# Cross-attention scores of a row tile: four chunks of 362 keys in two halves, or three chunks of 484 with a maximum each

## The chip, the cores and the metric

The kernel runs on one core of a Trainium2 chip. Its metric is the device time of one execution in microseconds; the median of three executions is compared. TensorE (PE) does the matrix products and transposes, VectorE (DVE) and ScalarE (ACT) work on what it leaves in PSUM, GpSimd (POOL) works in SBUF only, and SyncE (SP) starts the transfers. The engines run their own instruction streams and meet at semaphores.

## What is computed

A pre-norm decoder block over 16 samples of 100 tokens, width 128: banded self-attention, cross-attention over 1444 context keys with 16 heads, and a mixture of 16 experts with top 2 and a shared expert. The change lies in the cross-attention:

```
Q = (x @ W_Q.T + b_Q) per head;  K, V = (ctx @ W_K.T + b_K), (ctx @ W_V.T + b_V)
scores = where(mask, -10000, Q K^T / 8)         # 16 x 16 heads x 100 queries x 1444 keys
x = x + softmax(scores) V @ W_out.T + b_out
```

## The kernel before

The key projection is folded into the queries, so that all heads share the 128-wide context as keys and as values. A sample's 1600 rows (100 queries by 16 heads) make 13 row tiles: `FT` = 12 of 128 rows and one of 64 (`probs_half`). The keys are padded to `SKP` = 1448 columns. Each number is split in a high and a low part (`_hi`, `_lo`, type fp32r), and three products stand for one.

For a row tile t:

- **score** (PE, `score`, L1019): scores go to four PSUM banks, 362 keys in each, in two halves of two banks. A half is six matmuls: hi by hi, hi by lo, lo by hi, for two banks each. 26 halves for a sample.
- **take** (DVE, L943): one instruction for a half adds the bias row (mask and a constant), negates into `probs`, and carries the minimum so far (`nmax`), 724 elements in a row. The second half starts from the first one's minimum. A small read of the accumulator follows each.
- **bias** (POOL, L824): made for tile t + 1 while tile t is scored; two buffers.
- **exp** (ACT, L880) over the 1448 elements, with their sum; **recip** (DVE, L950) of the sum; **norm** (POOL, L836) multiplies the row by it.
- **step** (PE): two tiles form a group (the last group has three), which is taken in steps: transposes of two key blocks (`turn`, L1036) to one of two banks, ACT copies them as the high part `pT_hi` (L889), DVE makes the low part `pT_lo` (L955), and three steps later PE multiplies them with the context (`values`, L1061). 42 steps for a sample. At a group's end ACT and DVE take its result (`oT_hi`, L895, and `oT_lo`, L961). The first `turn` of group g waits until all its tiles are normalized.
- **prep** and **project**: queries and keys of the next sample, and the output projection of the one before.

All of it is one software pipeline over samples. `period()` writes out the order of one period by hand: steps 27 to 41 of the sample before, then steps 0 to 26 of this one, spread by their costs over the range 0 to 1; scores spread evenly in it (half n at (n + 0.5)/26); then preps at given places. PE follows that list. The lists of the other engines are the same with offsets in entries of it: exp at 1.5 entries after the last score entry of its tile, recip at 3.6, norm at 4.6, a take at 0.2 after its score, `pT_lo` at 0.5 after its step. Every engine works its list strictly in order. The hardware loop holds two periods (`odd` 1 and 0); its loads and register waits are repeated for each.

The end and the beginning of a period read, on PE, before: ... step 25, score 12.1, step 26 | step 27, score 0.0, step 28, score 0.1, step 29, step 30, score 1.0 ... (score t.h is half h of tile t). Step 30 is the first of the group with tiles 10, 11 and 12 of the sample just scored. Within a step PE first multiplies (values of three steps before), then transposes.

After the cross-attention come the experts (L1536 to L1552 are their matmuls, 400 columns each).

## Time and profile before

| | |
|---|---|
| median of 3 executions | 1850.08 us (1842.12 to 1850.58) |
| profiled execution, span from first to last instruction | 1843.5 us |
| around the span | no time of the profiled execution by itself is shown; the median of the runs is 6.6 us above its span |
| cross-attention, first to last score | 134.8 to 1485 us |
| PE busy, and DVE, ACT, POOL | 93%, 68%, 53%, 53% of the span |

Matmul records have an estimated end, so what a matmul costs is read from one start to the next. "xN" in a timeline row are N instructions in a row, with the start of the first. In brackets stands how long the engine was idle before, and what ended that.

### The profile page before, as it was taken

The numbers are of one execution on the slowest core, as the hardware profiler recorded it, in microseconds if no ns is written. First come the engines' busy times: TensorE is split into PE (matmuls) and PEld (weight loads), VectorE is DVE, ScalarE is ACT, GpSimd is POOL, SyncE is SP. The second block draws the span as 40 slices with busy tenths as digits, with TensorE's granted clock in tenths as the row PEclk, the third lists the DMA queues.
The fourth block names the chain that finished last, engine by engine and source line by source line (L and its number), as shares of the span: only waits on it lengthen the run. The fifth ranks groups of instructions, "written<-read, shape, count | busy, mean of one in ns | idle before, by whom it ended". The sixth has DMA issues, their size and how long they took to land. (4 is left out here: it accounts for less than half of the span.)

```text
span 1843.5 us, 37864 instructions
## 1 busy us (share of the span) xinstructions
PE 1708.8 (93%) x11436; PEld 1611.8 (87%) x11436; DVE 1262.3 (68%) x2678; ACT 978.6 (53%) x1763; POOL 975.0 (53%) x838
## 2 busy tenths in 40 slices
PE   5569999999999999999999999999999985899998
PEld 5448999989999998999899989999999974888887
DVE  5727776757676766677676757675767645788887
ACT  1216555646555655555555646464655532566665
POOL 0037565646465655556465646464656410666665
PEclk9769999999999999999999999999999996999999
DMA  5032010101010111101010101010100001222221
GB/s 84 1 92 62 25 52 29 45 30 48 31 48 27 51 36 41 49 29 48 27 52 29 47 27 48 31 48 27 51 29 29 24 22 55 79 79 79 79 79 44
DMA packets 89712, 83.69 MB, mean 45 GB/s; under 512 B 16003, under 2 KB 87069, under 8 KB 89519
## 3 DMA queue, kind: packets, MB, share of 16 engines
q1 hardware_dynamic: 82816, 79.03, 13.7%
q10 hardware_dynamic: 6703, 2.28, 0.9%
q8 instruction: 98, 1.61, 0.3%
q14 instruction: 95, 0.78, 0.1%
HBM read 77.08 MB, written 4.21 MB: 44 GB/s over the span
## 5 line engine op out<-in xcount | busy, mean ns | idle before, releaser
L955 DVE TENSOR_TENSOR pT_lo<-banks,pT_hi 128x512 fp32r<-128x512 f32 (+1 forms) x672 | 420.2, 631 | 307.1 <-ACT pT_hi L889 304.0
L889 ACT CAST pT_hi<-banks 128x512 fp32r<-128x512 f32 (+1 forms) x672 | 361.1, 543 | 429.2 <-PE banks L1036 422.2
L836 POOL TENSOR_SCALAR probs<-probs,row_inv 128x1448 f32<-128x1448 f32 x192 | 283.8, 1478 | 245.6 <-DVE row_inv L950 245.4
L824 POOL TENSOR_SCALAR bias<-mask,c_cur 128x1444 f32<-128x1444 uint8 x192 | 283.0, 1474 | 201.7 <-DVE nmax L943 189.0
L1036 PE MATMUL banks<-ident,probs 128*128 128x128 f32 x2304 | 363.3, 273 | 10.2 <-POOL probs_half L836 8.2
L1061 PE MATMUL banks<-pT_hi,ctx_hi 128*128 128x256 f32 (+1 forms) x1152 | 358.2, 311 | 12.8 <-DVE pT_lo L955 12.3
L1061 PE MATMUL banks<-pT_hi,ctx_lo 128*128 128x256 f32 (+1 forms) x1152 | 331.5, 288 | 0.0
L1061 PE MATMUL banks<-pT_lo,ctx_hi 128*128 128x256 f32 (+1 forms) x1152 | 330.1, 287 | 0.0
L880 ACT ACTIVATE probs<-probs,nmax 128x1448 f32<-128x1448 f32 x192 | 289.8, 1509 | 36.7 <-DVE nmax L943 36.7
L1036 PEld LDWEIGHTS banks<-ident,probs 128*128 128x128 f32 x2304 | 275.2, 141 | 15.9 <-issue 11.4
L1291 POOL TENSOR_TENSOR gated<-hid,gate_rows 128x400 f32<-128x400 f32 x144 | 172.1, 1202 | 145.7 <-DVE hid L1470 144.7
L1019 PE MATMUL banks<-ctxT_hi,qh 128*128 128x362 f32 x832 | 242.8, 373 | 4.4 <-POOL ql L858 2.8
L1061 PEld LDWEIGHTS banks<-pT_hi,ctx_hi 128*128 128x128 f32 x1152 | 219.8, 191 | 24.2 <-issue 14.5
L1061 PEld LDWEIGHTS banks<-pT_lo,ctx_hi 128*128 128x128 f32 x1152 | 219.3, 190 | 0.0
L1061 PEld LDWEIGHTS banks<-pT_hi,ctx_lo 128*128 128x128 f32 x1152 | 218.5, 190 | 0.0
L1019 PE MATMUL banks<-ctxT_hi,ql 128*128 128x362 f32 x832 | 207.7, 331 | 0.0
L1019 PE MATMUL banks<-ctxT_lo,qh 128*128 128x362 f32 x832 | 207.5, 331 | 0.0
L943 DVE CUSTOM_DVE_ANT_0 probs<-banks,bias,nmax 128x724 f32<-128x724 f32 x192 | 185.1, 964 | 14.2 <-PE banks L1019 12.8
L943 DVE CUSTOM_DVE_ANT_0 probs<-banks,bias 128x724 f32<-128x724 f32 x192 | 174.1, 907 | 27.4 <-PE banks L1019 16.5
L1461 DVE TENSOR_TENSOR h_lo<-gated,h_hi 128x400 fp32r<-128x400 f32 x144 | 133.1, 925 | 38.1 <-ACT h_hi L1350 38.0
L1019 PEld LDWEIGHTS banks<-ctxT_lo,qh 128*128 128x128 f32 x832 | 149.6, 191 | 0.0
L1019 PEld LDWEIGHTS banks<-ctxT_hi,ql 128*128 128x128 f32 x832 | 149.3, 191 | 0.0
(207 smaller groups left out, 2802.2 us busy)
## 6 DMA issues: line engine op xcount, KB each, us to landing
mask<-in_mask_BxSxS_bk SPq DMA_DIRECT2D x192, 180.5 KB
gate_rows<-gates_dram SPq DMA_DIRECT2D x18, 800.0 KB, 4.1
nat<-in_ctx SPq DMA_DIRECT2D x16, 704.0 KB
w_raw<-in_L_ffn_W SPq DMA_DIRECT2D x48, 128.0 KB, 2.1
mask_half<-in_mask_BxSxS_bk SPq DMA_DIRECT2D x16, 90.2 KB
xt<-in_x SPq DMA_DIRECT2D x4, 200.0 KB
x_dram<-xt SPq DMA_DIRECT2D x4, 200.0 KB
n2hi_dram<-n2hi SPq DMA_DIRECT2D x4, 200.0 KB
```

What stands on the lines that cost most here:

```text
L824: pool.tensor_scalar(bias[(t + i) % 2][0:n, 0:SK], src[:, :], MASKED, c_cur[i][0:n, t:t + 1], ALU.mult, ALU.add).then_inc(bias_ready, 1)
L836: pool.tensor_scalar(prob(j)[0:n, :], prob(j)[0:n, :], rinv[0:n, s:s + 1], 1.0, ALU.mult, ALU.mult).then_inc(probs_ready, 1)
L880: act.activation(prob(j)[0:n, :], prob(j)[0:n, :], ACT.Exp, bias=nmax[0:n, 1, s:s + 1], scale=-1.0, accum_out=rsum[0:n, s:s + 1]).then_inc ...
L889: act.copy(pT_hi[tslot(i, j)][:, 0:w], banks[:, T_BANK + j % 2, 0:w]).then_inc(turned_hi, 1)
L943: dve.tensor_tensor_reduce(prob(t)[0:n, cs].rearrange("p (a k) -> p a k", a=2), src, bias[(t + i) % 2][0:n, cs].rearrange("p (a k) -> p a ...
L955: dve.tensor_tensor(pT_lo[tslot(i, j)][:, 0:w], banks[:, T_BANK + j % 2, 0:w], pT_hi[tslot(i, j)][:, 0:w].bitcast(F32), ALU.subtract)\
L1019: last = pe.matmul(banks[:, S_BANK + c, 0:CW], qpart[:, rows], kpart[:, c * CW:(c + 1) * CW], start=first, stop=qpart is ql[i])
L1036: last = pe.transpose(banks[:, T_BANK + j % 2, at_col:at_col + r], prob(t)[0:r, c0:c0 + 128], ident[0:r, 0:r])
L1061: last = pe.matmul(banks[:, out_bank(g), 0:w], stationary[:, k, :], moving[tslot(i, j)][:, cs], start=(k == 0 and stationary is ctx_hi[i] ...
L1291: pool.tensor_tensor(gated[:, n % 4, :], hid[n % 2][:, :], gate_rows[odd][:, c * CT:(c + 1) * CT], ALU.mult).then_inc(gated_done, 1)
L1461: dve.tensor_tensor(h_lo[bodd][:, m, cs], gated[:, bn % 4, :], h_hi[bodd][:, m, cs].bitcast(F32), ALU.subtract).then_inc(hlo_done, 1)
```

## The change

A row tile's scores are taken in three parts of 484, 482 and 482 keys instead of two halves of 724. Each part lies in one bank, and the parts go round four banks. PE issues three matmuls for a part (nine for a tile, twelve before), and each part has a take of its own with its own `nmax` column. PE may start part n when part n - 4 is taken (before: half n when half n - 2 is taken); at the first two parts of every second sample, where the bank numbering starts anew, it waits for more. Scores are now 39 entries of the period instead of 26, which has 93 entries instead of 80; the offsets of exp, recip and norm stay 1.5, 3.6 and 4.6 entries after the tile's last score entry.

```diff
-CW = 362
-SKP = 4 * CW
+PARTS = [slice(0, 484), slice(484, 966), slice(966, 1448)]
+NP = len(PARTS)
+SKP = 1448
...
-    for n in range(2 * NT):
-        out.append(((n + 0.5) / (2 * NT), "score", 0, n))
+    for n in range(NP * NT):
+        out.append(((n + 0.5) / (NP * NT), "score", 0, n))
...
-        if kind == "score" and j % 2:
-            out.append((n + 1.5, "exp", db, j // 2))
+        if kind == "score" and j % NP == NP - 1:
+            out.append((n + 1.5, "exp", db, j // NP))
...
-            if j % 2:
-                out.append((n + 3.6, "recip", db, j // 2))
+            if j % NP == NP - 1:
+                out.append((n + 3.6, "recip", db, j // NP))
...
-        if kind == "score" and j % 2:
-            out.append((n + 4.6, "norm", db, j // 2))
+        if kind == "score" and j % NP == NP - 1:
+            out.append((n + 4.6, "norm", db, j // NP))
...
-        nmax = sb("nmax", [128, 2, PSLOTS + 1])
+        nmax = sb("nmax", [128, NP, PSLOTS + 1])
...
+        S_BANKS = 4
+
+        def score_bank(b_odd, n):
+            return S_BANK + (NP * NT * b_odd + n) % S_BANKS
...
-                            cs = slice(half * 2 * CW, (half + 1) * 2 * CW)
-                            src = banks[0:n, S_BANK + 2 * half:S_BANK + 2 * half + 2, 0:CW]
-                            first = -PAD if half == 0 else nmax[0:n, 0, s:s + 1]
+                            cs = PARTS[part]
+                            src = banks[0:n, score_bank(i, j), 0:cs.stop - cs.start]
+                            first = -PAD if part == 0 else nmax[0:n, part - 1, s:s + 1]
...
-                    wait(pe, scores_taken, b, 2 * NT, n - 1)
+                    wait(pe, scores_taken, b, NP * NT, n - 1 if i == 0 and n < 2 else n - S_BANKS + 1)
+                    cs = PARTS[part]
                     for qpart, kparts in ((qh[i], (ctxT_hi[i], ctxT_lo[i])), (ql[i], (ctxT_hi[i],))):
                         for kpart in kparts:
                             first = qpart is qh[i] and kpart is ctxT_hi[i]
-                            for c in (2 * half, 2 * half + 1):
-                                last = pe.matmul(banks[:, S_BANK + c, 0:CW], qpart[:, rows],
-                                                 kpart[:, c * CW:(c + 1) * CW], start=first, stop=qpart is ql[i])
+                            last = pe.matmul(banks[:, score_bank(i, n), 0:cs.stop - cs.start], qpart[:, rows],
+                                             kpart[:, cs], start=first, stop=qpart is ql[i])
                     last.then_inc(scores_ready, 1)
```

The waits on `scores_taken` and `scores_ready` of the other engines count 39 for a sample instead of 26, in the same sense.

## Rows read from the trace of the kernel before

**Rows 1.** The page: busy us, share of the span and instructions of each engine.

```profile
PE 1708.8 (93%) x11436; PEld 1611.8 (87%) x11436; DVE 1262.3 (68%) x2678; ACT 978.6 (53%) x1763; POOL 975.0 (53%) x838
```

**Rows 2.** Busy time by engine in two consecutive periods; clock, DMA share, GB/s last.

```profile
398.00:482.00 84.00, 83.91 (x605) 80.57 (x605) 59.22 (x136) 48.56 (x86) 49.85 (x41) 1.00 0.13 40
482.00:570.00 88.00, 85.44 (x604) 81.89 (x603) 59.30 (x135) 48.48 (x86) 49.87 (x41) 0.98 0.13 39
```

**Rows 3.** Waits over the whole span: us in total, times, longest us.

```profile
PE banks L1061 <- DVE pT_lo L955: 12.3, 6, 2.2
PE banks L1036 <- POOL probs_half L836: 8.2, 7, 2.2
```

**Rows 4.** Timeline at a period's change inside the loop: PE alone.

```profile
805.29 0.58 PE L1019 MATMUL banks<-ctxT_hi,qh 128*128 128x362 f32 x2
...
806.37 0.28 PE L1061 MATMUL banks<-pT_hi,ctx_hi 128*128 128x256 f32 x1
...
807.08 0.60 PE L1036 MATMUL banks<-ident,probs 128*128 128x128 f32 x4
807.43 0.57 PE L1019 MATMUL banks<-ctxT_hi,qh 128*128 128x362 f32 x2
807.84 0.49 PE L1019 MATMUL banks<-ctxT_lo,qh 128*128 128x362 f32 x2
...
808.51 0.28 PE L1061 MATMUL banks<-pT_hi,ctx_hi 128*128 128x256 f32 x1
```

**Rows 5.** Timeline of PE among the experts: seven matmuls of 400 columns.

```profile
1701.17 0.34 PE L1536 MATMUL banks<-t_hi,w_hi 128*128 128x400 f32 x1
...
1702.44 0.34 PE L1551 MATMUL banks<-h_lo,w_hi 128*128 128x400 f32 x1
```

**Rows 6.** Groups by line and shape: count, busy us, mean ns of one.

```profile
L955 DVE TENSOR_TENSOR pT_lo<-banks,pT_hi 128x512 fp32r<-128x512 f32 x480 | 327.4, 687 | 194.3 <-ACT pT_hi L889 191.2
L943 DVE CUSTOM_DVE_ANT_0 probs<-banks,bias,nmax 128x724 f32<-128x724 f32 x192 | 185.1, 964 | 14.2 <-PE banks L1019 12.8
L943 DVE CUSTOM_DVE_ANT_0 probs<-banks,bias 128x724 f32<-128x724 f32 x192 | 174.1, 907 | 27.4 <-PE banks L1019 16.5
L955 DVE TENSOR_TENSOR pT_lo<-banks,pT_hi 128x320 fp32r<-128x320 f32 x192 | 92.8, 490 | 112.8 <-ACT pT_hi L889 112.8
...
L943 DVE DVE_READ_ACCUMULATOR2_ANT nmax<- 128x1 f32 x384 | 31.8, 83 | 0.0
```

**Rows 7.** Timeline of the same change of period: the last score and what follows it.

```profile
801.98 0.58 PE L1019 MATMUL banks<-ctxT_hi,qh 128*128 128x362 f32 x2
...
803.77 0.60 PE L1036 MATMUL banks<-ident,probs 128*128 128x128 f32 x4
...
804.13 0.95 DVE L943 CUSTOM_DVE_ANT_0 probs_half<-banks,bias,nmax 64x724 f32<-64x724 f32 x1
...
805.13 1.51 ACT L880 ACTIVATE probs_half<-probs_half,nmax 64x1448 f32<-64x1448 f32 x1
...
805.64 0.41 DVE L961 TENSOR_TENSOR oT_lo<-banks,oT_hi 128x256 fp32r<-128x256 f32 x1
...
807.84 0.90 DVE L943 CUSTOM_DVE_ANT_0 probs<-banks,bias 128x724 f32<-128x724 f32 x1
...
808.66 0.15 DVE L950 RECIPROCAL row_inv<-row_sum 64x1 f32<-64x1 f32 x1
...
810.26 0.28 PE L1061 MATMUL banks<-pT_hi,ctx_lo 128*128 128x256 f32 x1
...
810.62 0.43 PE L1036 MATMUL banks<-ident,probs 128*128 128x128 f32 x2
```

**Rows 8.** Timeline where the loop starts anew (the period before that one).

```profile
718.43 0.38 PE L1061 MATMUL banks<-pT_hi,ctx_hi 128*128 128x256 f32 x1 [2.20 <-DVE pT_lo L955]
...
719.93 0.42 DVE L961 TENSOR_TENSOR oT_lo<-banks,oT_hi 128x256 fp32r<-128x256 f32 x1 [2.35 <-issue]
...
726.49 0.43 PE L1036 MATMUL banks<-ident,probs 128*128 128x128 f32 x2 [1.64 <-POOL probs_half L836]
```

More of the change, by code:

```diff
@@ L173, in pool_order @@
     for n, kind, db, j in ORDER:
-        if kind == "score" and j % 2 == 0:
-            t = j // 2 + 1
+        if kind == "score" and j % NP == 0:
+            t = j // NP + 1
             out.append((n + 0.5, "bias", db if t < NT else db + 1, t % NT))
-        if kind == "score" and j % 2:
-            out.append((n + 4.6, "norm", db, j // 2))
+        if kind == "score" and j % NP == NP - 1:
+            out.append((n + 4.6, "norm", db, j // NP))
         elif kind == "prep" and j >= 3:
@@ L820, in make_bias @@
                             wait(pool, mask_half_in, b + db, 16, 16)
-                        wait_apart(pool, scores_taken, b + db, 2 * NT, 2 * (t - 1), passed_pool)
+                        wait_apart(pool, scores_taken, b + db, NP * NT, NP * (t - 1), passed_pool)
                         src = masks[t % MSLOTS] if t < FT else mask_half
@@ L877, in emit @@
                             n, s = rows_of(j), slot(j)
-                            wait(act, scores_taken, b + db, 2 * NT, 2 * j + 2)
+                            wait(act, scores_taken, b + db, NP * NT, NP * j + NP)
                             act.activation(prob(j)[0:n, :], prob(j)[0:n, :], ACT.Exp,
-                                           bias=nmax[0:n, 1, s:s + 1], scale=-1.0,
+                                           bias=nmax[0:n, NP - 1, s:s + 1], scale=-1.0,
                                            accum_out=rsum[0:n, s:s + 1]).then_inc(exp_done, 1)
@@ L923, in emit @@
                         if kind == "score":
-                            t, half = j // 2, j % 2
+                            t, part = j // NP, j % NP
                             n, s = rows_of(t), slot(t)
-                            if half == 0:
+                            if part == 0:
                                 wait(dve, bias_ready, b + db, NT, t + 1)
@@ L935, in emit @@
                             else:
-                                wait(dve, scores_taken, b + db, 2 * NT, j)
-                            wait_apart(dve, scores_ready, b + db, 2 * NT, j + 1, passed_dve)
-                            cs = slice(half * 2 * CW, (half + 1) * 2 * CW)
-                            src = banks[0:n, S_BANK + 2 * half:S_BANK + 2 * half + 2, 0:CW]
-                            first = -PAD if half == 0 else nmax[0:n, 0, s:s + 1]
+                                wait(dve, scores_taken, b + db, NP * NT, j)
+                            wait_apart(dve, scores_ready, b + db, NP * NT, j + 1, passed_dve)
+                            cs = PARTS[part]
+                            src = banks[0:n, score_bank(i, j), 0:cs.stop - cs.start]
+                            first = -PAD if part == 0 else nmax[0:n, part - 1, s:s + 1]
                             dve.tensor_tensor_reduce(
-                                prob(t)[0:n, cs].rearrange("p (a k) -> p a k", a=2), src,
-                                bias[(t + i) % 2][0:n, cs].rearrange("p (a k) -> p a k", a=2), -1.0, first,
-                                ALU.add, ALU.min, nmax[0:n, half, s:s + 1]).then_inc(scores_taken, 1)
+                                prob(t)[0:n, cs], src, bias[(t + i) % 2][0:n, cs], -1.0, first,
+                                ALU.add, ALU.min, nmax[0:n, part, s:s + 1]).then_inc(scores_taken, 1)
                         elif kind == "recip":
@@ L1006, in score @@
                 def score(b, i, n):
-                    t, half = n // 2, n % 2
+                    t, part = n // NP, n % NP
                     rows = slice(t * 128, (t + 1) * 128)
```

## The prediction

> **What bounds the kernel now.** I read the page first: PE is busy 93% of the span, the next engine, DVE, 68% [rows 1]. A busy PE need not be a full PE, so I cut the span into periods of one sample. One takes 84 us, with PE busy 83.9 of them; the next takes 88 with PE busy 85.4, and TensorE's clock is 1.00 and 0.98 of full [rows 2]. So the even kind is work of PE from end to end, and the odd kind has some 4 us more. The list of waits says what they are: PE waited for DVE's `pT_lo` six times in the whole run, 12.3 us, and for the norm of `probs_half` seven times, 8.2 us [rows 3]. Those are the turns of the loop, where engines have nothing to run for a while (DVE's 2.35 us end with "issue" [rows 8]). Elsewhere the low parts are always made in time. A change of this kernel is therefore worth what it does to PE's own stream, and to the few places where PE stands; all else is hidden until it makes PE stand.
>
> **PE's stream.** A score matmul of 362 columns starts 0.1675 us after the one before: (808.51 - 807.84)/4 [rows 4]. With 256 columns it is (807.08 - 806.37)/6 = 0.118 [rows 4], with 400 columns, three after one another into the same bank, (1702.44 - 1701.17)/7 = 0.181 [rows 5]. Going from 256 to 400 adds 0.44 ns a column, so nearly all of the price is columns, and the change leaves those alone: 12 x 362 and 484 + 482 + 482 three times are both 4344. What is saved is the fixed part of three matmuls. A matmul of 484 columns is not in the trace. Bounds: in proportion to 362 columns 0.224; with the slope from 362 to 400, 0.36 ns a column, 0.212. I take 0.220, a little above the 0.219 that is in proportion to 400 columns, its nearest row. For a tile: 12 x 0.1675 = 2.010 before, 9 x 0.220 = 1.98 after, 0.03 less; for 208 tiles 6 us less (bounds: nothing, and 21 us less). Every matmul has a weight load of the same size, and at 256 columns these still fit into 0.118 [rows 4]; fewer of them save nothing by themselves.
>
> The Trainium skill ("TensorE: Matmul & The Clock Gate", Back-to-back issue gap) gives N/2.4 + 2.5 ns for an isolated gap; an estimate by it is 153 and 204 ns, some 8 ns less for a tile, 2 us in all. The same section states about 81 ns at 128 columns and 131 at 512 in a real stream; the rows of 362 and 400 columns disagree with that, and by it the change would be worth tens of microseconds, which is the second rival.
>
> The switch between transposes and split products costs 1.08 - 6 x 0.1675 = 0.08 us after each `turn`, whoever comes next [rows 4]; there are 42 turns in a period before and after, so 13 more score entries add no switch. Four banks give PE three parts ahead, so its own wait on `scores_taken` is not tighter, save for the first parts of every second sample. There part 0.0 needs part 12.1 taken, which by the chain below may be some 0.3 us late; it precedes the stall told next and is mostly taken back out of that.
>
> **DVE.** A take of 724 costs 907, or 964 ns if it starts from a maximum, and each is followed by a read of the accumulator (83 ns). `pT_lo` shows the price per element, (687 - 490)/192 = 1.03 ns [rows 6]. So 484 cost 907 - 240 x 1.03 = 0.66 us, and 482 with a maximum 964 - 242 x 1.03 = 0.715. For a tile: 0.66 + 2 x 0.715 + 3 x 0.083 = 2.34 after, 0.907 + 0.964 + 0.166 = 2.04 before. That is 0.3 us more for each of 208 tiles, 63 us of DVE in all; in a period DVE goes from 59 to 63 of 84 us [rows 2]. The cover is its idle time, 25 us a period, and parts come more evenly than halves did, about one between two steps. Behind a take on DVE stands the next `pT_lo`, and PE waits for that at the second step after. I price it at nothing; if the cover is gone at one step of every period it costs what is missing there, some 0.5 us, 8 us in all.
>
> **The one chain without slack.** Step 30 transposes the group of tiles 10 to 12, and tile 12 was scored last. In the undisturbed change of period PE's last value product starts at 810.26, the transposes would follow 0.12 later, and they start at 810.62: 0.24 late, for the norm [rows 7]. The links are: the take of 12.1 starts 804.13, exp 1.00 later, at 805.13; the take of 0.0 at exp + 2.71 (it stands on DVE behind `pT_lo` of step 27, which stands behind exp on ACT), recip at exp + 3.53, the transposes, with the norm on POOL between, at recip + 1.96 [rows 7].
>
> Now the new order, worked out from the fractions: ... step 25, score 12.1, step 26, score 12.2 | 0.0, step 27, 0.1, step 28, 0.2, step 29, step 30. The last score has moved behind step 26, and 0.0 ahead of step 27. Count PE from the start of 12.2. A part is 0.66, after a turn 0.74; a step after a score 1.06 (807.43 - 806.37), its values alone 0.71 [rows 4]. The transposes of step 30 come due at 0.74 + 0.66 + 1.06 + 0.74 + 1.06 + 0.74 + 1.06 + 0.08 + 0.71 = 6.85. Before, they came due 8.64 - 0.24 = 8.40 after the start of 12.1 at 801.98 [rows 7]. The deadline is 1.55 us nearer.
>
> The chain shortens less. The take of 12.2 stands on DVE behind `pT_lo` of step 26 and the `oT_lo` that ends group 3 there. `oT_lo` ends 806.05 - 803.77 = 2.28 after the start of step 26's transposes [rows 7], and those start 0.35 before part 12.2, so the take starts at 1.9, exp 0.75 later (a shorter take) at 2.65. Recip's offset, 3.6 entries, now puts it behind the take of 0.1, not of 0.0; that take is 0.2 shorter, so recip is at exp + 3.35 and the transposes at exp + 5.3 = 7.95. They are 1.1 late instead of 0.24. Bounds: if the take of 12.2 goes ahead 0.4 us sooner, 0.7; if 0.1 waits once more behind something, 1.8. I take 0.85 more in each undisturbed period, eight with the last sample: 7 us.
>
> At the loop's turn the same chain carries DVE's stop as well: 2.35 us before `oT_lo`, another before the take of 0.0, and PE then waits 1.64 us for the norm [rows 8]. By the sum of waits that is 8.2/7 = 1.2 us each [rows 3]. Of the nearer deadline 0.85 stays here too unless the stop hits elsewhere; with PE's own stop (2.20 [rows 8]) it is partly covered. I take 0.7, seven times, 5 us, between nothing and 1.5. Filling the pipeline at sample 0, where takes stand close together, costs four tiles of 0.3 us, 1 us.
>
> **Sum.** -6 + 7 + 5 + 1 = +7 us on a span of 1843.5, 1850.5. The median of the runs lies 6.6 above that profile's span, and I put the same on top: 1857 us, 0.4% more. A measurement of this kernel tells a change from none at about 0.5%, 9 us.
>
> **The rivals.**
> - *The stall does not grow* (chance 0.2). If recip gets ahead on DVE or PE runs late by itself, only the matmul term is left: -6 to 0, so 1844 to 1850. For it: PE only has to be 0.85 late on its own anywhere in steps 27 to 29. Against it: the order lists.
> - *Matmuls are paid by the piece* (0.14). Faster, 1830 to 1843. The mechanism: the fixed part of a score matmul is larger than the slope says. At 0.212 a tile saves 0.10 us, 21 us in all; with the stall it is 1841 to 1843 (-21 + 13), without it down to 1830. It decides if 484 columns take less than about 0.213. For it: the slope between 362 and 400 columns. Against: 256 columns, where three fewer would save almost nothing by proportion. In the extreme, with spacing set by the weight loads, three fewer of 0.1675 would be 0.5 us a tile, 104 us; the 0.118 of 256 columns, loads of the same size, exclude it. The stream figures of the Trainium skill (the section named above) point this way.
> - *DVE and ACT fall behind at several steps* (0.18). The transposes of a step need the `pT_lo` of the turn before last. With a touching pair of long steps between, the time from one turn to the turn after next is 0.35 + 0.74 + 1.06 + 0.08 + 0.71 = 2.94; the low part is there 805.64 - 803.77 = 1.87 after its turn [rows 7], and an exp of 1.5 on ACT ahead of it makes that 3.4, 0.4 late. Pairs 29/30, 32/33, 35/36, 38/39 and 41/0 now touch. At 0.4 us for three or four of them in a period it is 20 to 26 us over 16 periods, 1870 to 1883. Against: every pair is followed by a score, and three touching steps, which the old order has twice, are gone.
> - *The clock drops at the larger stall* (0.05). It is 1.00 in a period with a stall of 0.24 and 0.98 in one with stops of over 2 us [rows 2]. 2% of 84 us for eight more periods is 14 us: 1871. The Trainium skill ("TensorE: Matmul & The Clock Gate", A second HAM failure mode: psum-queue depth-cycling) tells of a kernel that went round PSUM banks and lost clock; here the periods already alternate between banks, at 1.00.
> - *My forecast* has 0.43, with 1850 to 1866 as its own range.
>
> **How the numbers follow.** Slower by over 0.5% (above 1859): the upper 0.4 of my case (0.17), and the third and fourth rival (0.23), 0.40. Faster (below 1841): most of the second rival (0.12), and the first where the matmul term is at its bound too (0.02), 0.14. Within 0.5%: the rest of my case (0.26), of the first rival (0.18) and of the second (0.02), 0.46. The range goes down to 1838, the middle of the second rival, and up to 1880, which cuts the upper part off the third; under 0.1 is left out at each end.
>
> **What would show it.** Starts of score matmuls 0.220 apart, nine for a tile. Takes of 0.66 and 0.715 us, DVE some 63 us busier. In an undisturbed change of period: take of 12.2, exp, takes 0.0 and 0.1, recip in this order, and the transposes of step 30 about 1.1 us after PE could; the wait of L1036 for the norm on 15 or 16 places instead of 7, some 20 us instead of 8.2. Wrong it would be by PE waits for `pT_lo` outside the turns of the loop, or by a matmul spacing below 0.215.

## The result, and the profile after

The changed kernel takes 1857.03 us (median of six runs, 1853.73 to 1859.56), the kernel before 1845.62 (six runs, 1842.12 to 1850.58). The ratio is 1.0049, with a 95% interval of 1.0031 to 1.0068: slower by 9 us by the ratio, by 11.4 between the two medians, just at the bound of what counts as a change here. The profiled spans are 1857.3 and 1843.5 us. The forecast of 1857 us hits the time, but by luck: it started from 1850.08, the median of three runs, where six runs give 1845.62, and it added 7 us where the medians differ by 11.4. Within the sum two terms were far off as well, one in each direction.

The page's line of busy times; it answers to [rows 1]:

```profile
PE 1713.6 (92%) x10812; PEld 1544.6 (83%) x10812; DVE 1293.0 (70%) x3094; ACT 971.6 (52%) x1763; POOL 974.3 (52%) x838
```

There are 624 fewer matmuls (3 for each of 208 tiles), and DVE is 31 us busier; PE's busy time did not fall. The groups by line and shape, which answer to [rows 6], give the price of the new takes:

```profile
L949 DVE CUSTOM_DVE_ANT_0 probs<-banks,bias,nmax 128x482 f32<-128x482 f32 x384 | 273.6, 712 | 9.9 <-DVE nmax L949 3.9 <-PE banks L1024 1.0
L949 DVE CUSTOM_DVE_ANT_0 probs<-banks,bias 128x484 f32<-128x484 f32 x192 | 126.0, 656 | 22.9 <-POOL bias L830 11.4 <-PE banks L1041 4.9 <-PE banks L1024 4.2
```

656 and 712 ns, against 0.66 and 0.715 us in the prediction. DVE's 31 us are half of the 63 forecast all the same, because the records of neighbouring instructions overlap. Where DVE does not wait, the instruction behind a take and its read starts 0.59 us after a take of 484 and 0.64 after one of 482, and before 0.84 and 0.89 us after the takes of 724 (medians). A tile costs 0.59 + 2 x 0.64 = 1.86 instead of 1.73, 0.13 more and not 0.3; 208 tiles make 28 of the 31 us.

To find the microseconds I cut both traces into periods, each from the first projection matmul of one sample to that of the next. Busy time by engine in three periods of the changed kernel, an undisturbed one and two that hold a turn of the loop (columns as in [rows 2]):

```profile
409.48:495.87 86.39, 84.56 (x569) 76.59 (x567) 61.24 (x162) 48.12 (x87) 49.84 (x42) 1.00 0.12 39
495.87:582.89 87.02, 84.55 (x568) 76.58 (x567) 61.05 (x162) 48.24 (x87) 49.78 (x42) 1.00 0.13 39
...
842.89:930.95 88.06, 85.93 (x568) 78.05 (x567) 61.27 (x162) 48.14 (x87) 49.77 (x42) 0.98 0.12 39
```

And of the kernel before, one undisturbed and three with a turn of the loop:

```profile
319.02:408.76 89.74, 85.69 (x605) 81.92 (x605) 59.31 (x135) 48.77 (x87) 49.84 (x42) 0.98 0.13 38
408.76:492.85 84.09, 84.00 (x606) 80.66 (x605) 59.30 (x135) 48.56 (x87) 49.84 (x42) 1.00 0.13 40
492.85:581.18 88.33, 85.77 (x605) 82.22 (x605) 59.32 (x135) 48.76 (x87) 49.88 (x42) 0.98 0.13 39
...
665.26:753.33 88.07, 84.24 (x606) 80.69 (x605) 59.31 (x135) 48.77 (x87) 49.83 (x42) 1.00 0.13 39
```

All seven undisturbed periods take 86.4 us where they took 84.1, and the last full one 86.21 against 83.86: 8 x 2.33 = +19 us. The six periods with a turn of the loop went the other way: 88.12, 87.02, 87.20, 88.06, 87.20 and 87.00 against 89.74, 88.33, 88.07, 88.11, 89.46 and 89.41, together 524.6 against 533.1, -9 us. The drain after them is 1.3 longer. To the end of cross-attention this makes +11.4, and the experts, which the change does not touch, took 2.4 more in this profile: 13.8, the difference of the spans.

**The undisturbed period.** The waits over the whole span, in total, times, longest (PE, then the weight loads), which answer to [rows 3]:

```profile
PE banks L1024 <- POOL ql L864: 24.5, 15, 2.8
...
PE banks L1041 <- POOL probs_half L842: 5.3, 14, 0.9
```

```profile
PEld banks L1024 <- DVE nmax L949: 27.5, 14, 2.4
...
PEld banks L1091 <- DVE qf L994: 13.4, 36, 1.0
...
PEld banks L1083 <- DVE oT_lo L966: 5.3, 14, 0.4
```

The wait of step 30 for the norm is there 14 times (15 or 16 were forecast), but small. The large one is new: PE stands ahead of a score (L1024), for POOL's `ql`. The timeline of an undisturbed change of period, which answers to [rows 7], shows where:

```profile
631.96 1.51 ACT L886 ACTIVATE probs<-probs,nmax 128x1448 f32<-128x1448 f32 x1 [0.91 <-DVE nmax L949]
632.26 0.46 PE L1024 MATMUL banks<-ctxT_hi,qh 128*128 128x482 f32 x1
632.56 0.38 PE L1024 MATMUL banks<-ctxT_lo,qh 128*128 128x482 f32 x1
632.78 0.38 PE L1024 MATMUL banks<-ctxT_hi,ql 128*128 128x482 f32 x1
633.00 0.28 PE L1066 MATMUL banks<-pT_hi,ctx_hi 128*128 128x256 f32 x1
...
633.41 0.37 DVE L994 TENSOR_TENSOR qf<-banks,qf 128x200 f32<-128x200 f32 x1
...
633.81 0.54 ACT L916 CAST qh<-qf 128x200 fp32r<-128x200 f32 x1 [0.25 <-DVE qf L994]
...
634.07 0.46 PE L1024 MATMUL banks<-ctxT_hi,qh 128*128 128x482 f32 x1
634.15 0.62 ACT L895 CAST pT_hi<-banks 128x512 fp32r<-128x512 f32 x1
634.59 0.38 PE L1024 MATMUL banks<-ctxT_hi,ql 128*128 128x482 f32 x1
634.81 0.69 DVE L960 TENSOR_TENSOR pT_lo<-banks,pT_hi 128x512 fp32r<-128x512 f32 x1 [0.96 <-ACT pT_hi L895]
635.49 0.71 POOL L864 TENSOR_TENSOR ql<-qf,qh 128x200 fp32r<-128x200 f32 x1
636.43 0.48 PE L1024 MATMUL banks<-ctxT_hi,qh 128*128 128x484 f32 x1 [1.46 <-POOL ql L864]
636.98 0.70 DVE L949 CUSTOM_DVE_ANT_0 probs_half<-banks,bias,nmax 64x482 f32<-64x482 f32 x1
637.73 1.51 ACT L886 ACTIVATE probs_half<-probs_half,nmax 64x1448 f32<-64x1448 f32 x1 [2.20 <-DVE nmax L949]
641.07 0.15 DVE L955 RECIPROCAL row_inv<-row_sum 64x1 f32<-64x1 f32 x1
642.55 0.28 PE L1066 MATMUL banks<-pT_hi,ctx_lo 128*128 128x256 f32 x1
643.03 0.43 PE L1041 MATMUL banks<-ident,probs 128*128 128x128 f32 x2 [0.20 <-POOL probs_half L842]
```

Part 12.1 starts at 632.26 behind a turn: 0.30 to its second matmul, then 0.22 apart, 0.74 in all, the forecast's price. Part 12.2 starts at 634.07. Part 0.0 would follow 0.22 after the last matmul of it (634.59); it starts at 636.43, 1.62 late. It reads the first low queries of the next sample, and the last piece of those is made on POOL from 635.49 to 636.2. Step 30 then loses another 0.36 (642.55 + 0.12 to 643.03). Together PE is 1.98 late at step 30, where it was 0.24: +1.74. The rounds of preparation for the next sample wait for DVE, which is busier now. Counted from one matmul's start to the next, this is 0.36 at the transposes of the second round (L1083, the 5.3 us of 14 places above, a wait that the kernel before does not have) and 0.25 and 0.17 ahead of two later ones (L1091, 13.4 us in 36 places; before it was 7.2 in 7). The output projection takes 0.14 more. That is 2.66; all the rest of PE's stream takes 0.33 less, near the 0.4 that the cheaper score matmuls were to give, and 2.33 is left.

**The turn of the loop.** DVE stops there longer than the releaser that the profile names accounts for: in the turn below, PE's half was written by 722.99 and the take starts 0.7 later. The kernel before stops twice: [rows 8] show 2.35 before `oT_lo`, and a second stop is ahead of the first take of tile 0. By the idle time in front of that take it is 2.0 to 2.5 us long in four of the six turns and 1.6 and 1.7 in two, and those two are the turns of 88.3 and 88.1 with only 2.3 to 2.6 us of idle PE; the turn of 88.07 has a long one, and its clock stayed. DVE, kernel before, in the same turn:

```profile
723.70 0.91 DVE L943 CUSTOM_DVE_ANT_0 probs<-banks,bias 128x724 f32<-128x724 f32 x1 [2.41 <-PE banks L1019]
...
724.54 0.15 DVE L950 RECIPROCAL row_inv<-row_sum 64x1 f32<-64x1 f32 x1
```

DVE, changed kernel, where this is the only stop (in each of its turns):

```profile
726.39 0.66 DVE L949 CUSTOM_DVE_ANT_0 probs<-banks,bias 128x484 f32<-128x484 f32 x1 [2.34 <-POOL bias L830]
...
728.21 0.15 DVE L955 RECIPROCAL row_inv<-row_sum 64x1 f32<-64x1 f32 x1
```

What goes on during these stops is in the view of the transfers. Between 714 and 730 us, in the same turn of the kernel before, it lists these beside the program's own:

```profile
q14 instruction: 5, 0.04, 0.8%
q8 instruction: 2, 0.03, 0.7%
```

They are loads of instructions. Those of q14, 8 KB each, start at 717.97, 717.99, 721.55, 721.60 and 723.94; DVE's stops run from 717.58 to 719.93 and from 721.29 to 723.70. In all 14 kernels of this document every one of these stops, 96 in 84 turns, ends 1.9 to 2.5 us after the start of such a transfer. So a wait for instructions is the likely cause. It is not shown, since no view says to which engine's stream a transfer belongs, and some of these transfers come without a stop.

The clock plays a part too. TensorE stops for 1.5 to 2.2 us in every turn; in some turns its clock then falls to half. Slices of 2 us after a turn of the kernel before (the column after POOL's is the granted clock):

```profile
544.00:546.00 2.00, 0.05 (x1) 0.06 (x1) 1.18 (x3) 1.87 (x3) 1.60 (x2) 1.00 0.02 8
546.00:548.00 2.00, 2.00 (x9) 2.00 (x10) 0.42 (x1) 0.18 (x2) 0.23 (x1) 0.50 0.07 17
548.00:550.00 2.00, 2.00 (x12) 2.00 (x10) 0.69 (x1) 0.58 (x1) 0.00 (x0) 0.65 0.27 92
550.00:552.00 2.00, 2.00 (x17) 2.00 (x16) 0.43 (x1) 0.59 (x1) 0.00 (x0) 1.00 0.01 4
```

After an all but empty slice PE runs for some 3 us at 0.50, 1.2 GHz, with 9 matmuls where 17 fit. Such a period has 85.7 us of busy PE instead of 84.24 (the rows of periods above), 1.5 more. Before, five of the six turns have it; after, two of six (the periods of 88.1), and those are the two with the longest stop of PE, 2.03 and 1.94 against 1.47 to 1.66 in the other four. Split by these rows, the 8.5 us that the six periods gained are 2.8 of busy time (512.9 to 510.0, the sum over the six) and 5.7 of idle time (20.2 to 14.6).

### The profile page after: what moved, and what is told of

Read it like the earlier page. It is cut to its first block and busy times, and to the rows that moved or that the text cites. A ratio compares the mean times of both kernels' runs of the same rounds, so it can differ in the third digit from the quotient of the medians.

```text
span 1857.3 us, 37583 instructions
## 1 busy us (share of the span) xinstructions
PE 1713.6 (92%) x10812; PEld 1544.6 (83%) x10812; DVE 1293.0 (70%) x3094; ACT 971.6 (52%) x1763; POOL 974.3 (52%) x838
## 3 DMA queue, kind: packets, MB, share of 16 engines
q10 hardware_dynamic: 6703, 2.28, 0.9%
## 5 line engine op out<-in xcount | busy, mean ns | idle before, releaser
L1066 PE MATMUL banks<-pT_hi,ctx_hi 128*128 128x256 f32 (+1 forms) x1152 | 343.2, 298 | 0.6 <-DVE ctxT_lo L980 0.6
L1024 PE MATMUL banks<-ctxT_hi,qh 128*128 128x482 f32 (+1 forms) x624 | 289.5, 464 | 25.8 <-POOL ql L864 24.5
L1041 PEld LDWEIGHTS banks<-ident,probs 128*128 128x128 f32 x2304 | 275.1, 140 | 13.8 <-issue 7.3
L949 DVE CUSTOM_DVE_ANT_0 probs<-banks,bias,nmax 128x482 f32<-128x482 f32 x384 | 273.6, 712 | 9.9 <-DVE nmax L949 3.9
L1024 PE MATMUL banks<-ctxT_hi,ql 128*128 128x482 f32 (+1 forms) x624 | 239.9, 384 | 0.0
L1024 PE MATMUL banks<-ctxT_lo,qh 128*128 128x482 f32 (+1 forms) x624 | 239.3, 384 | 0.0
L1024 PEld LDWEIGHTS banks<-ctxT_hi,qh 128*128 128x128 f32 x624 | 119.3, 191 | 41.2 <-DVE nmax L949 27.5
L949 DVE CUSTOM_DVE_ANT_0 probs<-banks,bias 128x484 f32<-128x484 f32 x192 | 126.0, 656 | 22.9 <-POOL bias L830 11.4
L1024 PEld LDWEIGHTS banks<-ctxT_hi,ql 128*128 128x128 f32 x624 | 118.2, 189 | 19.2
```

What stands on the lines that cost most here:

```text
L949: dve.tensor_tensor_reduce(prob(t)[0:n, cs], src, bias[(t + i) % 2][0:n, cs], -1.0, first, ALU.add, ALU.min, nmax[0:n, part, s:s + 1]).the ...
L1024: last = pe.matmul(banks[:, score_bank(i, n), 0:cs.stop - cs.start], qpart[:, rows], kpart[:, cs], start=first, stop=qpart is ql[i])
L1041: last = pe.transpose(banks[:, T_BANK + j % 2, at_col:at_col + r], prob(t)[0:r, c0:c0 + 128], ident[0:r, 0:r])
L1066: last = pe.matmul(banks[:, out_bank(g), 0:w], stationary[:, k, :], moving[tslot(i, j)][:, cs], start=(k == 0 and stationary is ctx_hi[i] ...
```

## The experiments

None of them changes what is computed. The times of one group stand against runs of the kernel before on the same chip. "Undisturbed" and "turn" are the lengths of the two kinds of period in the profile, from the starts of the first projection matmuls: 84.1 and 88.9 (mean) before, 86.4 and 87.4 after. Line numbers are those of the changed kernel, except in the kernels made from the one before.

**1. The order at the change of period.** First the last score ahead of step 26, and the first of the next sample behind step 27, as these stood in the old order:

```diff
-        out.append(((n + 0.5) / (NP * NT), "score", 0, n))
+        out.append(((n + 0.5) / (NP * NT) + 0.001 * ((n == 0) - (n == NP * NT - 1)), "score", 0, n))
```

> The kernel after, with two neighbours exchanged in the written order at each end of the period: part 12.2 ahead of step 26 again, part 0.0 behind step 27 again, as the halves stood in the kernel before. Nothing else moves. Theory 1 (the order at the change of period is the cost): an undisturbed period falls from 86.4 us to 84.5 to 85, part 0.0 finds the last low queries ready, the transposes of step 30 are some 0.6 late instead of 2.1 in all; over 15 periods 15 to 20 us less than after, partly given back where the loop turns: 1838 to 1846, ratio to before 0.995 to 1.0. Theory 2 (the cost is the three shorter takes on DVE, 0.3 us a tile, wherever they stand): the order matters little, 1854 to 1858, ratio 1.004 to 1.006.

Measured: 1852.24 us, ratio 1.0034 (1.0021 to 1.0046), undisturbed 86.01. PE's wait for `ql` is gone, the one at step 30 is back. Timeline of the same change of period:

```profile
635.47 1.51 ACT L886 ACTIVATE probs_half<-probs_half,nmax 64x1448 f32<-64x1448 f32 x1 [1.59 <-DVE nmax L949]
...
638.96 0.15 DVE L955 RECIPROCAL row_inv<-row_sum 64x1 f32<-64x1 f32 x1
...
640.93 0.43 PE L1041 MATMUL banks<-ident,probs 128*128 128x128 f32 x2 [0.85 <-POOL probs_half L842]
```

The reciprocal comes 3.49 after exp, and PE stands about 1.0. The order of scores and steps on PE explains only 0.4 of the 2.3 us: the theory that it is the whole cause missed its 84.5 to 85, and the time lies between the ranges of both theories. The second kernel moves only the first part of the next sample:

```diff
+        out.append(((n + 0.5) / (NP * NT) + 0.001 * (n == 0), "score", 0, n))
```

> The kernel after, with only part 0.0 moved back behind step 27. After, PE stands 1.6 us at part 0.0 for the low queries made on POOL, and 0.36 us more at the transposes of step 30 for the norm of tile 12. Theory 1a (the norm's chain of tile 12 sets the sum of both, and the wait at part 0.0 lies inside it): the wait at 0.0 shrinks to about 0.5, that at step 30 grows by the same, the period stays at 86.4: 1854 to 1858. Theory 1b (the wait at 0.0 is a cost of its own): 1.1 us less a period, 10 to 15 us less: 1842 to 1847. Theory 2 (takes): unchanged too, but then also in the run with both exchanged.

Measured: 1846.66 us, 1.0000 (0.9987 to 1.0012), undisturbed 85.50. This undoes 9 us with one entry, but it is no clean test, because moving the entry also moves the exp of tile 12, which hangs on the same position, behind ACT's high part of step 27. The reciprocal then comes 2.07 after exp instead of 3.35. That gave the next theory: it is the place of exp on ACT that matters.

**2. Is it the low queries themselves?** If `ql` is late by accident, making it earlier cures the wait at 0.0; if PE must wait for the chain of tile 12 anyway, the wait only moves.

```diff
-            out.append((n + 1.6, "prep", db, j))
+            out.append((n + 1.4, "prep", db, j))
```

> The kernel after, with POOL's low queries one place earlier in its list (offset 1.4 instead of 1.6 entries), so that those of the last round go ahead of the norm of tile 11 instead of behind it. They are then there about 1.4 us earlier. Theory 1a (norm chain of tile 12 sets the sum): the wait at part 0.0 falls in the periods where it waits for nothing else, in the others it stays since the banks start anew there and part 12.1 is taken late; what falls comes back at step 30; 1854 to 1858. Theory 1b (the wait for the low queries is the cost): 1.3 us less in at least every second period, 1842 to 1849.

Measured: 1856.42 us, 1.0052 (1.0035 to 1.0069), undisturbed 86.42. The timeline:

```profile
636.15 0.49 PE L1024 MATMUL banks<-ctxT_hi,qh 128*128 128x484 f32 x1 [1.20 <-DVE nmax L949]
...
643.02 0.32 PE L1041 MATMUL banks<-ident,probs 128*128 128x128 f32 x1 [0.47 <-POOL probs_half L842]
```

0.0 starts 0.28 earlier and now waits for its bank, that is for the take of 12.1; step 30 starts at 643.02, in the changed kernel at 643.03. To take the bank's wait away as well, the fifth kernel rotates over three banks straight through, so that 0.0 does not need the take of part 12.1:

```diff
-        S_BANKS = 4
+        S_BANKS = 3
...
-                    wait(pe, scores_taken, b, NP * NT, n - 1 if i == 0 and n < 2 else n - S_BANKS + 1)
+                    wait(pe, scores_taken, b, NP * NT, n - S_BANKS + 1)
```

> The kernel after with both things taken away that part 0.0 waits for: the parts go round three banks, so that the numbering does not start anew (PE may start a part when the one three before is taken, in every sample), and the last low queries go ahead of the norm of tile 11 on POOL. Order of PE, DVE and ACT unchanged. Theory 1a (the norm chain of tile 12, take 12.2, exp, high and low part of step 27, take 0.1, recip, norm, sets the sum): the wait at part 0.0 shrinks below 0.5 us and the one at step 30 grows to 1.5 to 2; undisturbed period still 86.2 to 86.5, time 1853 to 1858. Theory 1b (waits at part 0.0 are a cost of their own): period 84.9, time 1840 to 1846.

Measured: 1857.63 us, 1.0051 (1.0035 to 1.0068), undisturbed 86.40. The timeline:

```profile
635.13 0.48 PE L1024 MATMUL banks<-ctxT_hi,qh 128*128 128x484 f32 x1 [0.37 <-POOL ql L864]
...
642.79 0.43 PE L1041 MATMUL banks<-ident,probs 128*128 128x128 f32 x2 [1.08 <-POOL probs_half L842]
```

The wait at 0.0 is 0.54 now, that at step 30 1.24; their sum is 1.78 where it was 1.98, and the period is what it was. The two waits are one: PE is held to the chain take of 12.2, exp, reciprocal, norm, and what it does not lose at 0.0 it loses at step 30.

**3. Is the order enough, without the thirds?** The kernel before with its halves, with the last half of tile 12 behind step 26 and the first half of tile 0 ahead of step 27, as in the change:

```diff
-        out.append(((n + 0.5) / (2 * NT), "score", 0, n))
+        out.append(((n + 0.5) / (2 * NT) + 0.0075 * ((n == 25) - (n == 0)), "score", 0, n))
```

> The kernel before, halves and all, with its last half moved behind step 26 and its first half ahead of step 27: the order that the change has at this place, and nothing of the change otherwise. Theory 1: the undisturbed period grows from 84.06 to 85.5 to 86.5, with a wait of PE at half 0.0 for the low queries and a later step 30; at the turns of the loop little or nothing is added: 1855 to 1866, ratio 1.005 to 1.01. Theory 2 (takes): 1843 to 1848, ratio 0.999 to 1.001.

Measured: 1856.79 us, 1.0059 (1.0042 to 1.0076): as slow as the whole change. Undisturbed 85.38, turns 88.07. PE waits at 0.0 for `ql`, in halves as in thirds:

```profile
635.24 0.60 PE L1019 MATMUL banks<-ctxT_hi,qh 128*128 128x362 f32 x2 [0.76 <-POOL ql L858]
```

The order alone costs 1.3 us in an undisturbed period, more than half of the change's 2.3. It also alters the turns: DVE stops there once, for 3.9 to 4.4 us, and they take 0.8 less than before.

**4. The place of exp.** Exp of tile 12 stands ahead of the high part of step 27 on ACT (1.5 us), that makes `pT_lo` late, and the reciprocal is behind this on DVE. The sixth kernel is the fifth with this exp later:

```diff
-            out.append((n + 1.5, "exp", db, j // NP))
+            out.append((n + (2.2 if j // NP == NT - 1 else 1.5), "exp", db, j // NP))
```

> The run with three banks and early low queries, and exp of tile 12 one place later on ACT, behind the high part of step 27 instead of ahead of it. exp then doesn't hold up the high part, the low part and the takes behind it, on which recip waits: recip comes at exp + 2.1 as in the run with part 0.0 moved back, not at exp + 3.35. Theory 1a: the chain is 1.3 us shorter, undisturbed period 85.0 to 85.4, 1840 to 1847. Theory 1b: no change against the run without this edit.

Measured: 1844.34 us, 0.9973 (0.9958 to 0.9989), undisturbed 84.95. The timeline:

```profile
634.15 1.51 ACT L886 ACTIVATE probs_half<-probs_half,nmax 64x1448 f32<-64x1448 f32 x1
...
635.77 0.15 DVE L955 RECIPROCAL row_inv<-row_sum 64x1 f32<-64x1 f32 x1
...
637.79 0.40 PE L1041 MATMUL banks<-ident,probs 128*128 128x128 f32 x2
```

The reciprocal follows exp by 1.62, just its duration and the read behind it, and PE does not wait at step 30. From the fifth kernel to this one the one number 2.2 takes 1.45 us off each undisturbed period and 13 us off the run. With 0.0 behind step 27 instead (the entry of the second kernel with three banks and early low queries):

> Part 0.0 behind step 27 again (its exp of tile 12 then stands behind the high part of step 27 by the offsets), three banks, early low queries. In the run with part 0.0 moved back alone, part 0.1 still waited 0.64 us for the take of 12.2 because the banks start anew there, and the transposes of step 30 had 0.4 to spare. Theory 1: that wait goes, undisturbed period 84.9 to 85.1 instead of 85.5, 1840 to 1845, ratio to before 0.996 to 1.0. What is left over 84.1 then belongs to waits of the preparation rounds for DVE, 0.3 us twice a period. Rival: the take of 12.2 is late whatever the banks, and what part 0.1 doesn't wait step 30 does: 1845 to 1848.

Measured: 1844.11 us, 0.9981 (0.9966 to 0.9996), undisturbed 85.13: the same within the intervals. And the same late exp in the kernel before:

```diff
-            out.append((n + 1.5, "exp", db, j // 2))
+            out.append((n + (2.2 if j // 2 == NT - 1 else 1.5), "exp", db, j // 2))
```

> The kernel before, with exp of tile 12 one place later on ACT, behind the high part of step 27. If exp ahead of that high part is what makes the chain to step 30 long there too, the 0.24 us of the undisturbed periods go (84.08 to 83.85) and some of the waits at the turns of the loop: 1838 to 1845, ratio 0.996 to 0.999. If the stop of DVE at the turn of the loop sets the chain there, only 0.24 in eight periods: 1843 to 1846, ratio 0.999 to 1.0.

Measured: 1844.18 us, 0.9983 (0.9968 to 0.9999), undisturbed 83.80, which is the 0.24 of step 30 gone and no more. The turns take 89.1.

**5. The two rounds of preparation.** In the changed kernel their positions move behind the DVE work that they waited for:

```diff
-    for r, at in enumerate((0.453, 0.493, 0.534, 0.588, 0.621, 0.701, 0.728, 0.774, 0.861, 0.888, 0.941)):
+    for r, at in enumerate((0.453, 0.493, 0.553, 0.588, 0.633, 0.701, 0.728, 0.774, 0.861, 0.888, 0.941)):
```

> The kernel after, with two preparation rounds moved behind the next score part on PE: round 2 from behind step 9 to behind part 7.0, round 4 from behind step 12 to behind part 8.0. In the kernel after, PE stands 0.3 us before round 2 for a low output made on DVE (oT_lo) and 0.29 us before round 4 for DVE's read of round 3, in every period; the kernel before stands at neither. Theory: these are a second place where shorter spacing meets a chain through DVE, and independent of the change of period: 0.5 to 0.6 us less in each of 15 periods, undisturbed period 85.8 to 85.9, 1847 to 1850. Rival (something later in the period takes the time back, as at the change of period): 86.4, 1855 to 1858.

Measured: 1853.44 us, 1.0033 (1.0018 to 1.0048), undisturbed 86.07: 0.33 of the 0.55 that I expected, and a time between the two ranges. The wait at L1083 is gone, another for `oT_lo` has appeared at L1091 (3.9 us in 15 places). With everything of the sixth kernel:

> The run with three banks, early low queries and exp of tile 12 one place later, and also the two preparation rounds moved behind the next part. Theory: both repairs add up, undisturbed period 84.95 - 0.55 = 84.4, 1834 to 1839, ratio to before 0.992 to 0.996. What is left over the 84.08 of before would be a wait of 0.56 at part 0.0, less 0.2 for the cheaper score matmuls. Rival (the period is bound by something else by then, as DVE's load of 63 of 84 us): above 84.8, 1842 to 1845.

Measured: 1838.67 us, 0.9953 (0.9937 to 0.9970), undisturbed 84.59, turns 86.8. This is the best of the thirds. In an undisturbed period the halves of the eighth kernel are still 0.8 shorter. The thirds win by the turns: all but one keep clock 1.00.

```profile
489.70:576.30 86.60, 84.12 (x569) 76.52 (x567) 60.85 (x162) 48.15 (x87) 49.87 (x42) 1.00 0.13 40
```

**6. Do thirds help at the turn, or only another place?** DVE's second stop is there in both kernels of halves looked at so far (before, and the eighth, there 2.4 to 2.7 us in four turns of six, 1.8 and 1.5 in the others) and in none of thirds; the fourth kernel, also of halves, has the one long stop. Thirds add instructions to DVE's stream, so the stop may depend on the takes or just on where in the stream the loop's instructions lie. To the eighth kernel, three waits that are always fulfilled ahead of each take:

```diff
+                            for _ in range(3):
+                                wait(dve, bias_ready, b + db, NT, t + 1)
```

> The halves kernel with exp of tile 12 one place later, and three more waits ahead of every take on DVE that are always fulfilled (78 in a period), so that DVE's loop is about as long in instructions as with thirds. At the turn of the loop DVE stops twice in every kernel with halves (2.2 and 1.2 to 2.1 us without an instruction) and once in every kernel with thirds (1.6 to 2.0), and the period there is 88.9 us against 87.4. Theory L (where the second stop falls, or if it does, depends on how DVE's instruction stream lies in the loop): the stops at the turn change, loop periods go to 87 to 88, time 1834 to 1841. Theory O (it depends on the order of the work at the turn, or on other engines): two stops as before, 1844 to 1848, the more waits costing nothing measurable elsewhere.

Measured: 1833.20 us, 0.9903 (0.9886 to 0.9919), just under the range of theory L, undisturbed 83.79, turns 86.0 to 87.7. And 40 such waits once, ahead of the pipeline, with the loop's own instructions as they were:

```diff
+                for _ in range(40):
+                    dve.wait_ge(zeroed, 1)
```

> The halves kernel with exp of tile 12 one place later, and 40 more always fulfilled waits on DVE once, ahead of the pipeline: the loop's instructions are the same, only their place in the stream is shifted. If the place alone sets the stops at the turn of the loop, they change (one, or of another length) and the time with them, 1836 to 1848; if the length of the loop or the work around it sets them, two stops as before and 1843 to 1846.

Measured: 1835.14 us, 0.9909 (0.9889 to 0.9928), just under the expected range too, undisturbed 83.79, turns 87.38, 87.76, 86.25, 87.71, 86.13 and 87.70. DVE at the turn of the eighth kernel:

```profile
717.96 0.42 DVE L961 TENSOR_TENSOR oT_lo<-banks,oT_hi 128x256 fp32r<-128x256 f32 x1 [2.31 <-issue]
...
722.00 0.91 DVE L943 CUSTOM_DVE_ANT_0 probs<-banks,bias 128x724 f32<-128x724 f32 x1 [2.58 <-PE banks L1019]
722.84 0.15 DVE L950 RECIPROCAL row_inv<-row_sum 64x1 f32<-64x1 f32 x1
```

And of the twelfth:

```profile
716.45 0.42 DVE L963 TENSOR_TENSOR oT_lo<-banks,oT_hi 128x256 fp32r<-128x256 f32 x1 [2.61 <-issue]
...
718.36 0.15 DVE L952 RECIPROCAL row_inv<-row_sum 64x1 f32<-64x1 f32 x1
```

From `oT_lo` to the reciprocal it is 4.88 us in the one and 1.91 in the other. No turn of the eleventh or twelfth has the second stop, though in the twelfth nothing in the loop has changed, so thirds are not what removes it; the place of the instructions is enough. The clock fell in four turns of six here, in six of six in the eighth kernel. In the sums of the six turns (534.6 to 522.9 us) idle time accounts for 7.6 us and PE's busy time for 4.1.

The eleventh and twelfth are the best versions: halves, exp of tile 12 later, DVE's stream shifted, 0.9% under the kernel before.

## Why the prediction came out as it did

**What held.** PE's own stream was the bound. The score matmul of 482 and 484 columns starts 0.22 after the one before, the value taken (0.220), so the rival "matmuls are paid by the piece", which needed 0.213 or less, is out. The stream figure of 131 ns at 512 columns that the Trainium skill gives ("TensorE: Matmul & The Clock Gate", Back-to-back issue gap), and that the rival leaned on, is not reached here at 482. Takes cost 656 and 712 ns. The chain beyond exp came to the hundredth: the reciprocal at exp + 3.34 (641.07 - 637.73; 3.35 forecast), the transposes at recip + 1.96. That the last score moves nearer to step 30, and that this costs more than the matmuls give, was the forecast's core; the kernel of halves in the changed order bears it out.

**The matmul term (-6 us).** By the spacing it is right. Over the seven undisturbed periods the starts are 0.1667 apart before and 0.2197 after, 0.02 a tile where 0.03 was forecast; all of PE's stream but its waits and the projection gives back 0.33 in a period. No period is shorter for it: with the waits taken out as far as I could, thirds are at 84.59 and halves at 83.80. Counted from start to start, thirds lose there 0.55 at part 0.0, 0.47 ahead of a preparation round and 0.14 in the output projection, and gain 0.36.

**The chain's start (the term of +7, measured 8 x 1.74 = 14).** The step that failed is "the take starts at 1.9". It started 2.91 after part 12.2 (636.98 - 634.07), so the lateness at step 30 was 2.0 and not 1.1. I had taken `oT_lo` of step 26 at the same distance behind its transposes as before, 2.28. But one entry of the order further up, two things now stand in front of step 25's high part on ACT, which starts 2.24 after its transposes instead of 1.24: exp of tile 11 (631.96, 1.5 us), and behind it `qh` of a preparation round, for which ACT waits another 0.25 until DVE has made `qf` (633.41). DVE has no gap from 630.60 to then; it works through low parts and the takes of 11.2 and 12.0. By the timeline the low parts, and the takes behind them, follow that high part one after another. Where I looked for what stands in front of the reciprocal I should have gone one exp further back, and looked at the preparation round too: taking exp of tile 11 away alone would not start the high part sooner. That exp of tile 12 is a link is shown by the sixth kernel; for exp of tile 11 and for `qf` it is read from the timeline only, and no run moves them.

**The missed wait.** The forecast names the wait of part 0.0 on `scores_taken`, puts it at some 0.3 and says that it is "mostly taken back" out of the stall at step 30. The wait that came last was for `ql`, which the part also needs and which the move made due sooner; it is not named. The bank was late too, and by more than 0.3: in the third kernel, with `ql` early, 0.0 still starts only 0.28 sooner. The reasoning about it was right, as the third and fifth kernels show: such a wait is part of the same 2 us. Hence the wrong picture of the waits (5.3 us for the norm instead of 20, and 24.5 for `ql`) costs nothing beside the term above.

**The cover of DVE (rival three).** "I price it at nothing" cost 0.78 us in a period, some 12 us over 15 periods, at three rounds of the preparation. It did so although DVE's added work was 31 us and not 63: the sum added up records that overlap. The rival had the mechanism, DVE late at several places, but put it at the touching pairs of steps and at 0.4 for each; in an undisturbed period no such pair waits long enough to enter the list of waits.

**The turns of the loop (+5, measured -9).** The wrong sign, and six of them, where the forecast counts seven. I took the stops as given and laid the nearer deadline on top. DVE's second stop vanished, and three turns kept their clock. Nothing in the forecast's reading of the order or the takes foretells either; for the stop the twelfth kernel shows that the place of the instructions is enough. The clock was kept where PE's stop was shorter than before (1.47 to 1.66 against 1.94 to 2.21); why it was shorter stays open. The undisturbed periods were forecast at about +4 (7, less half of the matmul term) and came to +19, the turns at about +3 and came to -9. Filling the pipeline cost nothing (first projection at 234.94 in both profiles) instead of 1, the drain 1.3 and the experts 2.4 that no term foresaw. The sum of +7 stands against 13.8 between the profiles and 11.4 between the medians. What brought it to 1857 is the base: the 6.6 us put on top of the span. In the runs on record a run's time is 1.7 above its own span (1859.01 and 1857.3), so 4.9 of the 6.6 were scatter between runs. The total was right by luck.

**The clock (rival four).** It did not drop in undisturbed periods with a wait of 1.62: 1.00 in each. The Trainium skill's failure mode for kernels that go round PSUM banks ("TensorE: Matmul & The Clock Gate", A second HAM failure mode: psum-queue depth-cycling) is not seen with four rotating banks.

**Open.** What DVE waits for at the turn of the loop, and why once or twice, was not settled; the loads of instructions at each stop are the best lead, and no run varies them by themselves. Whether the clock falls after PE's stop is not explained by the length of the stop alone. Over the kernels here the falls mostly follow the longer stops, but the turn of [rows 8] has a stop of 2.20 us and the one at 544 of 2.11, and the clock stays 1.00 in the first. Why the output projection takes 0.14 us more was not looked into.

## What to carry to other kernels

When an order is derived from fractions, changing the number of pieces moves every entry that hangs on them: list, for each dependent stage, what now stands in front of it on its engine, two steps back along the chain, and look up every operand that a moved instruction needs, not only the one with a bank. If one chain sets the time, its waits are one sum wherever they show; the cure is the position of the one long instruction in front of its links (here exp, one number, 13 us). A change of 0.5% in a looped kernel must be compared by kind of period, since the turns of the loop can shift by more than that for reasons that have nothing to do with it (here the run by 0.7%, from the eighth kernel to the twelfth).

## What was not expected of the hardware

- DVE stops once or twice at a turn of the loop: before, 2.3 to 2.6 us the first time and 1.6 to 2.5 the second. Whether there is a second stop changed with the place of its instructions alone: 40 fulfilled waits ahead of the loop took the mean turn from 89.1 to 87.2 us, and the run from 0.9983 to 0.9909 of the kernel before.
- After a stop of about 2 us PE's clock either stays at 1.00 or falls to 0.50 for some 3 us, which costs 1.5 us: it fell in five turns of six before, two of six after, six of six in the eighth kernel, four of six in the twelfth. In the changed kernel it fell after the two longest stops; in the kernel before it stayed once after 2.20 us and fell once after 1.94.
- Each of these stops ends 1.9 to 2.5 us after a transfer of 8 KB of instructions starts. That the one waits for the other is not shown.
- A wait that is always fulfilled, three times ahead of each take, cost nothing that could be seen: undisturbed periods of 83.79 us with and without.
